# Summing 25 half blocks of the row degrees with accumulating DMAs on GpSimd's queue, in a new block order with 29 instead of 39 whole blocks

## The reference, cut to what matters

```python
# layer 0
deg = jnp.clip(jnp.sum(adj, axis=1, keepdims=True), 1.0)
x = _layernorm(x + (x @ W_self + (adj @ x / deg) @ W_neigh))
# layer 1: one product
x = _layernorm(x + relu(adj @ (x @ kernel) + bias))
# layer 2: two products, layer 3: two products with swish
```

## Time and profile before

| | |
|---|---|
| median of 3 runs | 1150.82 us (1150.64 to 1151.54) |
| the profiled execution: its time | 1149.44 us |
| its span (first to last instruction) | 1147.3 us, 2.14 us lie around it |
| PE / DVE / ACT / POOL busy in the span | 99% / 72% / 48% / 6% |
| share of PE in the chain that ended last | 98% |

### The profile page before, as it was taken

One profiled execution on the slowest core, in us unless ns is written; L12 is line 12 of the kernel. 1 busy time (PEld: TensorE's weight loads), 2 busy tenths in 40 slices (PEclk: granted clock), 3 DMA queues, 4 the chain that ended last, 5 costly groups with the idle time before them and its releaser, 6 DMA issues.

```text
span 1147.3 us, 13933 instructions
## 1 busy us (share of the span) xinstructions
PE 1134.8 (99%) x4968; PEld 894.9 (78%) x4968; DVE 827.3 (72%) x1109; ACT 550.5 (48%) x624; POOL 70.6 (6%) x49
## 2 busy tenths in 40 slices
PE   8999999999999999999999999999999999999997
PEld 3455767778788888888888888888888888888886
DVE  6878879899799666585545388666668454677887
ACT  1112334444565444474444375444457444566875
POOL 0000000000121111000000000000000000000121
PEclk9999999999999999999999999999999999999999
DMA  9987666665768656596655586666659665787885
GB/s 348 339 310 271 230 227 231 217 231 186 286 249 301 213 190 213 170 342 239 214 204 189 181 303 251 228 208 206 222 186 341 207 200 190 250 332 275 310 275 180
DMA packets 82642, 279.45 MB, mean 244 GB/s; under 512 B 8848, under 2 KB 14224, under 8 KB 82576
## 3 DMA queue, kind: packets, MB, share of 16 engines
q1 hardware_dynamic: 76288, 273.97, 67.6%
q10 hardware_dynamic: 6288, 4.59, 1.3%
HBM read 276.43 MB, written 2.10 MB: 243 GB/s over the span
## 4 chain that ended last, share of the span: by engine, by line
PE 98%; DVE 1%; DMA 0%; ACT 0%; issue 0%; SPq 0%
PE acc L456 27%; PE acc L461 27%; PE acc L457 27%; PE acc L444 12%; PE acc L493 4%; PE acc L471 1%; PE acc L479 1%; DMA raw<-adj_tiles 0%; ACT t_x L600 0%; DVE adj_lo L797 0%; DVE x_rows L767 0%; DVE stats L694 0%; DVE stats L675 0%; DVE t_y L691 0%; PE acc L506 0%; DVE t_y L744 0%
## 5 line engine op out<-in xcount | busy, mean ns | idle before, releaser
L797 DVE TENSOR_TENSOR adj_lo<-raw,adj_hi 128x1024 fp32r<-128x1024 f32 x419 | 509.8, 1231 | 254.1 <-ACT adj_hi L644 239.7
L644 ACT CAST adj_hi<-raw 128x1024 fp32r<-128x1024 f32 x419 | 438.6, 1051 | 400.3 <-PE acc L461 246.9
L456 PE MATMUL acc<-adj_hi,op_hi 128*128 128x512 f32 x1336 | 529.7, 396 | 0.0
L457 PE MATMUL acc<-adj_hi,op_lo 128*128 128x512 f32 x1336 | 520.4, 390 | 0.0
L461 PE MATMUL acc<-adj_lo,op_hi 128*128 128x512 f32 x1336 | 411.7, 389 | 0.2 <-DVE adj_lo L797 0.2
L456 PEld LDWEIGHTS acc<-adj_hi,op_hi 128*128 128x128 f32 x1336 | 251.0, 188 | 53.5 <-issue 3.1
L457 PEld LDWEIGHTS acc<-adj_hi,op_lo 128*128 128x128 f32 x1336 | 251.0, 188 | 53.3 <-issue 3.1
L461 PEld LDWEIGHTS acc<-adj_lo,op_hi 128*128 128x128 f32 x1336 | 250.7, 188 | 53.3 <-DVE adj_lo L797 0.6
L664 DVE TENSOR_TENSOR deg_part<-deg_part,raw 128x1024 f32<-128x1024 f32 x120 | 146.6, 1222 | 19.6 <-DMA raw<-adj_tiles 15.3
L444 PE MATMUL acc<-raw,x_rows 128*128 128x512 f32 x312 | 139.6, 599 | 5.3 <-DMA raw<-adj_tiles 5.3
L820 POOL TENSOR_TENSOR rstd<-var_eps,minus_half 128x4 f32<-128x4 f32 x31 | 56.5, 1822 | 1063.6 <-DVE var_eps L680 1063.6
(11 more groups left out here) (60 smaller groups left out, 301.7 us busy)
## 6 DMA issues: line engine op xcount, KB each, us to landing
raw<-adj_tiles SPq DMA_DIRECT2D x518, 512.0 KB, 4.8
x_rows<-x_blocks SPq DMA_DIRECT2D x8, 256.0 KB, 5.7
xt<-x_t ACTq DMA_DIRECT2D x8, 256.0 KB, 4.7
out<-t_x ACTq DMA_DIRECT2D x7, 256.0 KB, 4.4
out<-xt SPq DMA_DIRECT2D x2, 128.0 KB, 1.9
w<-W ACTq DMA_DIRECT2D x2, 64.0 KB, 5.0
b<-b ACTq DMA_DIRECT2D x2, 64.0 KB, 7.1
w_res<-W_self ACTq DMA_DIRECT2D x1, 64.0 KB, 4.0
```

The costliest lines, as they stand in the source:

```text
L456: nc.tensor.matmul(bank, op_block(op_hi, p, j), a_hi, start=first and b == 0, stop=False)
L457: nc.tensor.matmul(bank, op_block(op_lo, p, j), a_hi, start=False, stop=False)
L644: nc.scalar.copy(split_hi(s), raw[:, g % RAW, :]).then_inc(hi_ready, 1)
L797: nc.vector.tensor_tensor(split_lo(s), raw[:, g % RAW, :], split_hi(s).bitcast(fp32), ALU.subtract).then_inc(lo_ready, 1)
```

## The change

- The block order of pass 0 is new: rows 0, 1 and 2 are worked on together, and 29 blocks are whole instead of 39, so 58 halves instead of 78; the other 20 become split halves. The number of halves used ahead stays 50, and so does the number of loads on SP's queue (518). The places in the lists of all engines are new for pass 0.
- Of the 128 halves of pass 0, 25 (4, 6, 7 and 8 halves of the rows 4, 5, 6 and 7) are no longer added by DVE. POOL loads them a second time, straight into `deg_part`: the first of a row with a plain DMA, the others with a DMA that adds to what lies there (`accum_op=ALU.add`). Each waits on POOL until the one before has landed. The first of a row also waits until PE has read the row that used the buffer before (`deg_rows_done`). DVE starts a row that has such halves only when all of them have landed (`deg_landed`).
- `POW_AT` says how many of these DMAs POOL issues ahead of the m-th `pow`.
- `deg_part` has three buffers, one per row modulo 3; the separate `deg_sum` is gone, the last addition is made in place and PE reads `deg_part`.
- The weight of the last layer is loaded into the buffer of `W_neigh` later, by ACT's queue.

```diff
@@ -47,6 +47,7 @@
     RAW = 6
     SPLIT = 9
     BANKS = 8
+    DEG_BUFS = 3
     EPS = 1e-5
     NORM = [0, 1, 3, 5]
 
@@ -55,21 +56,22 @@
 
 
     ONE, BOTH, FIRST, SECOND, WHOLE = range(5)
-    FIRST_ORDER = (
-        [(0, i, q, WHOLE) for q in range(7) for i in (0, 1)]
-        + [(0, 0, 7, WHOLE)] + [(0, 2, q, WHOLE) for q in range(5)] + [(0, 1, 7, WHOLE)]
-        + [(0, 2, 5, WHOLE), (0, 3, 3, WHOLE), (0, 2, 6, WHOLE), (0, 3, 4, WHOLE), (0, 3, 5, WHOLE), (0, 2, 7, WHOLE)]
-        + [(0, 3, 0, BOTH), (0, 3, 6, WHOLE), (0, 3, 1, BOTH), (0, 4, 4, WHOLE), (0, 4, 0, BOTH), (0, 3, 7, WHOLE),
-           (0, 3, 2, BOTH), (0, 4, 5, WHOLE), (0, 4, 1, BOTH), (0, 4, 6, WHOLE), (0, 4, 2, BOTH), (0, 5, 5, WHOLE),
-           (0, 5, 0, BOTH), (0, 4, 7, WHOLE), (0, 4, 3, BOTH)]
-        + [(0, 5, 1, BOTH), (0, 5, 6, WHOLE), (0, 5, 2, BOTH), (0, 5, 3, BOTH),
-           (0, 5, 7, WHOLE), (0, 5, 4, BOTH)]
-        + [(0, 6, 6, WHOLE), (0, 6, 0, BOTH), (0, 6, 1, BOTH), (0, 6, 2, BOTH), (0, 6, 7, WHOLE), (0, 6, 3, BOTH),
-           (0, 6, 4, BOTH), (0, 6, 5, BOTH)]
-        + [(0, 7, q, BOTH) for q in range(5)]
-        + [(0, 7, q, FIRST) for q in range(5, 7)] + [(0, 7, 7, WHOLE)] + [(0, 7, q, SECOND) for q in range(5, 7)]
-        + [(1, 2, 2, ONE), (1, 3, 3, ONE), (1, 4, 4, ONE)]
-    )
+    FIRST_ORDER = [
+        (0, 2, 2, WHOLE), (0, 0, 0, WHOLE), (0, 0, 2, WHOLE), (0, 2, 3, WHOLE), (0, 0, 3, WHOLE), (0, 1, 6, WHOLE),
+        (0, 1, 3, WHOLE), (0, 2, 0, WHOLE), (0, 1, 5, WHOLE), (0, 0, 4, WHOLE), (0, 1, 1, WHOLE), (0, 2, 6, WHOLE),
+        (0, 2, 5, WHOLE), (0, 2, 1, WHOLE), (0, 1, 0, WHOLE), (0, 1, 4, WHOLE), (0, 1, 2, WHOLE), (0, 6, 1, FIRST),
+        (0, 0, 1, ONE), (0, 0, 7, WHOLE), (0, 0, 6, WHOLE), (0, 0, 5, ONE), (0, 5, 6, WHOLE), (0, 5, 5, ONE),
+        (0, 6, 2, FIRST), (0, 1, 7, WHOLE), (0, 2, 7, WHOLE), (0, 4, 0, BOTH), (0, 7, 7, ONE), (0, 3, 7, WHOLE),
+        (0, 3, 1, BOTH), (0, 3, 3, WHOLE), (0, 2, 4, ONE), (0, 3, 5, WHOLE), (0, 3, 0, BOTH), (0, 4, 6, WHOLE),
+        (0, 4, 1, BOTH), (0, 5, 3, FIRST), (0, 3, 2, BOTH), (0, 4, 4, ONE), (0, 6, 1, SECOND), (0, 4, 7, ONE),
+        (0, 6, 0, FIRST), (0, 3, 6, WHOLE), (0, 3, 4, WHOLE), (0, 6, 0, SECOND), (0, 5, 2, FIRST), (0, 5, 7, WHOLE),
+        (0, 6, 2, SECOND), (0, 4, 2, BOTH), (0, 4, 3, BOTH), (0, 4, 5, ONE), (0, 7, 3, BOTH), (0, 7, 2, BOTH),
+        (0, 5, 1, BOTH), (0, 6, 7, ONE), (0, 5, 3, SECOND), (0, 5, 4, FIRST), (0, 6, 5, FIRST), (0, 5, 0, FIRST),
+        (0, 5, 0, SECOND), (0, 5, 4, SECOND), (0, 6, 3, FIRST), (0, 6, 3, SECOND), (0, 7, 0, BOTH), (0, 6, 4, BOTH),
+        (0, 6, 6, ONE), (0, 7, 4, FIRST), (0, 6, 5, SECOND), (0, 7, 5, BOTH), (1, 3, 3, ONE), (0, 5, 2, SECOND),
+        (0, 7, 4, SECOND), (0, 7, 1, FIRST), (0, 7, 6, FIRST), (0, 7, 6, SECOND), (1, 2, 2, ONE), (0, 7, 1, SECOND),
+        (1, 4, 4, ONE)
+    ]
     NEXT_ORDER = (
         [(0, 1, 1, ONE), (0, 2, 1, ONE), (0, 0, 0, ONE), (0, 5, 5, ONE), (0, 1, 0, ONE), (0, 5, 6, ONE),
          (0, 2, 0, ONE), (0, 5, 7, ONE), (0, 4, 4, ONE)]
@@ -123,12 +125,21 @@
 
     SPLIT_NO = {g: s for s, g in enumerate(g for g in range(TOTAL) if not STEPS[g][4])}
     SPLIT_STEP = list(SPLIT_NO)
-    DEG_NO = {g: d for d, g in enumerate(g for g in range(TOTAL) if STEPS[g][0] == 0)}
+
+    LANDED = [0, 0, 0, 0, 4, 6, 7, 8]
+    LANDINGS = [g for r in range(CHUNKS) for g in [g for g in range(TOTAL) if STEPS[g][:2] == (0, r)][:LANDED[r]]]
+    DEG_NO = {g: d for d, g in enumerate(g for g in range(TOTAL) if STEPS[g][0] == 0 and g not in LANDINGS)}
     DEG_FIRST = {STEPS[g][1]: g for g in reversed(DEG_NO)}
     DEG_LAST = {STEPS[g][1]: g for g in DEG_NO}
     EARLY_NO = {g: e for e, g in enumerate(g for g, ahead in PRODUCTS if ahead)}
     LAST_USE = {g: at for at, (g, ahead) in enumerate(PRODUCTS)}
-    RESIDUAL_FROM = max(DEG_NO) + 1
+
+    X_FIRST = {}
+    for g in range(TOTAL):
+        if STEPS[g][0] == 0 and STEPS[g][2] not in X_FIRST.values():
+            X_FIRST[g] = STEPS[g][2]
+    X_ORDER = list(X_FIRST.values())
+    RESIDUAL_FROM = max(g for g in range(TOTAL) if STEPS[g][0] == 0) + 1
     SUM_OF = [(STEPS[g][0] + ahead, STEPS[g][1]) for g, ahead in PRODUCTS]
     BEGUN = {}
     ENDED = {}
@@ -159,63 +170,66 @@
 
     PARTS = 8
     ROWS_AT = [
-        21, 36, 47, 62, 81, 105, 125, 153
+        21, 53, 60, 80, 108, 125, 149, 166
     ]
     DEGREES_AT = [
-        30, 41, 53, 74, 98, 117, 145, 173
+        46, 53, 71, 101, 118, 142, 157, 176
     ]
     WEIGHT_AT = [
-        32, 43, 57, 76, 100, 120, 148, 176, 192, 196, 200, 220, 238, 260, 278, 304, 318, 322, 326, 348, 366,
+        48, 55, 75, 103, 120, 144, 161, 178, 192, 196, 200, 220, 238, 260, 278, 304, 318, 322, 326, 348, 366,
...
     X_HI_AT = [
-        422, 423, 424, 425, 426, 427, 429, 430
+        271, 272, 273, 274, 275, 276, 277, 342
     ]
...
     SUM_AT = [
-        431, 435, 470, 574, 710, 798, 950, 1062, 1174, 1214, 1238, 1342, 1422, 1518, 1598, 1694, 1790, 1822,
+        374, 451, 558, 742, 822, 910, 998, 1086, 1182, 1214, 1238, 1342, 1422, 1518, 1598, 1694, 1790, 1822,
...
     X_LO_AT = [
-        6, 38, 70, 102, 134, 166, 198, 230
+        6, 22, 54, 86, 134, 150, 166, 374
     ]
     RDEG_AT = [
-        270, 366, 462, 574, 694, 790, 918, 1054
+        390, 446, 582, 726, 814, 918, 990, 1070
     ]
     BIAS_AT = [
-        294, 382, 478, 582, 710, 806, 934, 1070, 1190, 1205, 1246, 1350, 1430, 1526, 1606, 1702, 1798, 1830,
+        414, 462, 590, 750, 830, 926, 1006, 1094, 1190, 1205, 1246, 1350, 1430, 1526, 1606, 1702, 1798, 1830,
...
     NORM_AT = [
-        310, 398, 486, 590, 718, 814, 942, 1086, 1204, 1222, 1262, 1366, 1446, 1542, 1622, 1718, None, None,
+        430, 486, 598, 766, 838, 942, 1022, 1110, 1204, 1222, 1262, 1366, 1446, 1542, 1622, 1718, None, None,
...
+    ]
+    POW_AT = [
+        0, 2, 7, 12, 17, 24, 25, 25
     ]
...
@@ -393,8 +410,8 @@
                 sp.dma_start(cols(x_rows, k), cols(x_blocks, k)).then_inc(x_loaded[k], 16)
 
             for g, (p, r, k, h, whole) in enumerate(STEPS):
-                if g % 4 == 0 and g // 4 < CHUNKS:
-                    load_x(g // 4)
+                if g in X_FIRST:
+                    load_x(k)
                 if g >= RAW:
                     before = g - RAW
                     if STEPS[before][4]:
@@ -476,8 +493,8 @@
                 pe.wait_ge(deg_ready, m + 1)
                 bank = take(("z", m))
                 for b in range(BPC):
-                    last = nc.tensor.matmul(bank[:, b:b + 1], deg_sum[:, b * P:(b + 1) * P], ones[:], start=True,
-                                            stop=True)
+                    last = nc.tensor.matmul(bank[:, b:b + 1], deg_part[:, FINISH[m][1] % DEG_BUFS, b * P:(b + 1) * P], ones[:],
+                                            start=True, stop=True)
                 last.then_inc(deg_rows_done, 1)
 
             def times_weight(m):
@@ -577,6 +597,9 @@
                     return
                 if u == SUM_AT[m]:
                     sum_out(m)
+                    if m == CHUNKS + 1:
+                        act.wait_ge(z_done, CHUNKS)
+                        act.dma_start(w_neigh[:], L3_W).then_inc(w_3_loaded, 16)
                 if p == 0 and u == SELF_AT[m]:
                     self_rows(m)
                 if p == 4 and u == SILU_AT[m]:
@@ -646,27 +669,30 @@
 
         @block.vector
         def _(dve):
-            def split_x(k):
-                dve.wait_ge(op_hi_ready, k + 1)
+            def split_x(n):
+                k = X_ORDER[n]
+                dve.wait_ge(op_hi_ready, n + 1)
                 nc.vector.tensor_tensor(op_cols(op_lo, 0, k), cols(x_rows, k), op_cols(op_hi, 0, k).bitcast(fp32),
                                         ALU.subtract).then_inc(op_ready, 1)
 
             def degree(g, r):
                 wait_raw(dve, g)
                 src = raw[:, g % RAW, :]
-                sums = deg_part[:, r % 2, :]
+                sums = deg_part[:, r % DEG_BUFS, :]
                 if g == DEG_FIRST[r]:
-                    if r > 1:
-                        dve.wait_ge(deg_ready, r - 1)
+                    if LANDED[r] > 0:
+                        dve.wait_ge(deg_landed, 16 * sum(LANDED[:r + 1]))
+                    elif r >= DEG_BUFS:
+                        dve.wait_ge(deg_rows_done, r - DEG_BUFS + 1)
+                if g == DEG_FIRST[r] and LANDED[r] == 0:
                     nc.vector.tensor_copy(sums, src).then_inc(deg_step, 1)
                 else:
-                    dve.wait_ge(deg_step, DEG_NO[g])
+                    if g != DEG_FIRST[r]:
+                        dve.wait_ge(deg_step, DEG_NO[g])
                     nc.vector.tensor_tensor(sums, sums, src, ALU.add).then_inc(deg_step, 1)
                 if g == DEG_LAST[r]:
                     dve.wait_ge(deg_step, DEG_NO[g] + 1)
-                    if r > 0:
-                        dve.wait_ge(deg_rows_done, r)
```

(66 more changed lines are left out.)

## The result

The changed kernel takes 1179.01 us (1174.86 to 1181.11), the kernel before beside it 1150.73 us; the ratio is 1.024, 95% interval 1.0217 to 1.0263. The profiled execution took 1179.74 us, its span is 1177.9 us.

A forecast was written before the change was run, and what follows sets the result against it. It took PE, busy 99% of the span, as the bound. Span 1147.3 less 7.1 plus 0.7 gave 1140.9 us, 2.14 more made 1143.0, and 1.4 to the median 1144.4 us; transfers cost nothing; range 1143.0 to 1164.

The forecast's parts named there:

- PE's work, 7.1 us: PE in pass 0: 20 whole halves become split ones, 1.717 us down to 1.36 each, 7.1 us less; the whole possible gain.
- x loads, 0.7 us: Chunk loads of x before step 21: seven instead of six, costing 0.7 us (range 0 to 0.7).
- DVE and ACT cost nothing: Beside PE in pass 0: DVE ends 4 us lighter, ACT 21 us heavier while half idle; cost nothing.
- The other moved waits: Last rows' use at product 188 and step 79's slot: nothing, with little cover; 1 to 2 us each if they fail.
- The cover of 85.9 us: PE's walk from product 101 to 158, 85.9 us, hides 15 serial transfers: 85.8 us available, 5.7 us each.
- The price of a transfer, 5.5 us: Each serial transfer on POOL's queue takes 5.5 us, bounds 3.8 to 8.0; 15 take 82.5 us and cost nothing.
- the two extras above 5.8: Upper bound of a transfer's price: 1.3 us if the destination is read, 0.9 if POOL is held behind DVE; 8.0 us.
- The looser places: Other transfer chains with more cover: row 5 8.0 us each, before step 104 6.9, two at step 74 7.2 (14.4 us).
- Rival 1: Transfers at 7.0 us outlast their cover, PE stands 19.2 us at steps 117 to 121: 1163.6 us; decides from 6.1; chance 0.19.
- Rival 2: DVE's lock on the SBUF ports in full: transfers of 8.0 us, 34.2 over the cover, 1178.6 us; chance 0.09 with beyond.
- the thick part's row: Profile row of same-size loads on SP's queue in dense traffic: 5.8 us from issue to landing, used in the upper bound.
- The rule on the port: DVE and GpSimd share SBUF ports; DVE's lock may hold GpSimd's descriptors, making a transfer 8.0 us; the page names 2-port modes.

## Why the prediction was wrong, point by point

- **PE's work, 7.1 us: right in the main.** Without the transfers PE is busy 1129.4 us against 1134.8, 5.4 less. The first 21 whole halves take 1.0 us longer (next point), which counts as busy; 0.7 us stay open. The time fell by 5.7 us where the sum had 6.4.
- **x loads, 0.7 us: too small by about 2.** The first weight stage of pass 1 comes at 313.83 instead of 318.29 us, 4.5 us earlier where 7.1 - 0.7 were counted. The first x stage is 1.0 us later than in the earlier trace rows (44.18 against 43.18), behind the same 21 whole halves, and PE waits 1.0 us for a rounding behind a load between 50 and 100 us, where the DMA engines are busy 0.93.
- **DVE and ACT cost nothing: right** in the new order; the trace without transfers shows 1.2 us of PE waiting for both.
- **The other moved waits** (product 188, step 79) cost nothing measurable: right.
- **The cover of 85.9 us: right.** Without transfers PE goes from the degrees of the fourth row (176.21 us) to the weight stage at 313.83 in 137.6 us. Plain ones, at 6.02 us, make it 145.5 (from 176.89 to 322.36), 7.9 more; the count gives 15 x 6.02 - 85.9 = 4.4. Adding ones make it 163.6 (185.25 to 348.87), 26.0 more; the count gives 15 x 7.30 - 85.9 = 23.6. The 2.4 to 3.5 us between weren't traced one by one; DVE catching up after a wait and the slower clock, both left out of the count, lie there.
- **The price of a transfer, 5.5 us: this is the step that failed**, and with it the sign. It measured 7.30 us, inside the bounds of 3.8 and 8.0 that were given, but the value taken was the row of another queue. The argument that a serial queue saves what the addition costs was wrong on both sides: alone, with nothing ahead of it, an adding transfer takes 5.60 us, already at the cover; beside loads a serial transfer is slowed all the same, a plain one from 3.80 to 7.35 us with six in flight and to 6.02 in the kernel. Of the two extras above 5.8, the 1.3 for a destination that has to be read was real (7.30 - 6.02 = 1.3 in the kernel), and the hold behind DVE, 0.9, was not. So the prediction's own rows gave 5.8 + 1.3 = 7.1, and it let the queueing that it expected to be absent cancel the 1.3.
- **The looser places were not loose.** For two transfers at step 74 the prediction allowed 14.4 us; they took 16.5, and began 4 us late, since row 4's four, which it didn't count, took 8.9 each (from 101.06 to 136.73 us). The stall of 5.0 us came there first, and the degrees of the fourth row are 9.0 us late (185.25 against 176.21). So a price of 7.3 alone wouldn't have saved the sum: with it the prediction's count gives 1168, and some 11 us are still missing, these 9.0 and the 2.4 of the cover's point.
- **The clock** had no term. 8.9 us of the 35.0 are PE's longer busy time, most of it behind its stalls, though part of this lies inside the time that the transfers set anyway.
- **Rivals.** Rival 1's mechanism was right, and its place in part (steps 117 to 121; more than half of the stall time was at 74 and 104). Its deciding point of 6.1 us fits the plain transfers: at 6.02 they took 1154.51 us. Rival 2 gave the right time, 1178.6 us, by luck: 8.0 us each with the hold behind DVE, which isn't there, in place of the late start and the clock, which it lacked. Its chance and rival 1's, 0.28 together, were too low for a price for which the thick part's row and the reading gave 7.1.
- **The rule on the port.** Beside DVE's two-tensor additions a transfer takes 5.62 us, alone 5.60: no hold. Beside fp32 copies its issue is held for all of them, 72.08 us. The Trainium skill (SBUF — State Buffer, "SBUF: two separate sides") ties the starved descriptors to 2-port modes, which an fp32 copy within SBUF triggers. The run agrees on which of the two holds the issue. The page puts the lock at the whole of one instruction; here the issue was held through 120 copies in a row.

## What to carry to other kernels

Before work is moved to a chain of serial transfers, count the chain against the bound engine's walk between the event that starts it and the one that needs it, and price a transfer of its own kind, under the loads that will run beside it; if only another queue's row is there, take the upper end. Short work that others wait for (here the powers) waits with such a chain when it stands behind it, so count it with the chain; placing it elsewhere on the same engine gained nothing here, and another engine wasn't tried. Leave room: 17 transfers with some 8 us each were hidden, 15 in 86 us cost 26. Idle time of a second engine is its lead; spend it only where no local wait uses it.
